# Gate logits from the raw rows with centred weights, gather norms on ScalarE, transposes inside products

## What is computed

```python
def moe(x):                                   # x: layer norm of the rows
    logits = x @ W_gate + b_gate              # 8 experts
    _, top_idx = top_k(logits, 2)
    y_all = relu(einsum('bsd,edh->bseh', x, W_e) + b_e)
    return take_along_axis(y_all, top_idx[..., None], axis=2).mean(axis=2)

x = x + 0.5 * moe(layernorm(x))
x = x + attention(layernorm(x))               # one head of width 128, softmax
x = x + 0.5 * moe(layernorm(x))
```

## Time and profile before

| what | value |
|---|---|
| runs, device time | median 271.39 us of 3 (270.65 to 272.92) |
| profiled execution, first to last instruction | 270.3 us; the median of the runs is 1.1 us above it |
| TensorE (PE) busy | 237.3 us, 88% |
| VectorE (DVE) busy | 168.9 us, 62% |
| GpSimd (POOL) busy | 118.9 us, 44% |
| ScalarE (ACT) busy | 103.1 us, 38% |
| chain that ended last | PE 59%, DVE 14%, DMA 10%, issue 6%, ACT 4% |
| mean granted TensorE clock | 0.985 of full |

### The profile page before, as it was taken

The page is one execution under the profiler, slowest core; times in us unless marked ns, Lnnn a source line. Parts: engine busy times, 40 slices in busy tenths (PEclk is TensorE's granted clock), DMA queues, the critical chain, the costliest instruction groups (busy, mean ns, idle before and its releaser), DMA issues.

```text
span 270.3 us, 4837 instructions
## 1 busy us (share of the span) xinstructions
PE 237.3 (88%) x1307; PEld 176.9 (65%) x1308; DVE 168.9 (62%) x413; ACT 103.1 (38%) x184; POOL 118.9 (44%) x137
## 2 busy tenths in 40 slices
PE   6687679998999999989999897789989999999940
PEld 2353258776888888658777575266766888888730
DVE  3659778976354444766788988837943454444691
ACT  1986825654333333313335325023432433333300
POOL 4300456755565652324232610332475666664240
PEclk9999999999999999999999999999999999999985
DMA  7999589743875456144402022162164445537995
GB/s 234 380 390 410 196 316 395 305 146 134 271 215 145 133 156 221 33 141 155 155 1 80 0 81 78 32 202 80 53 219 136 157 130 157 163 128 203 347 333 197
DMA packets 22789, 49.38 MB, mean 183 GB/s; under 512 B 4332, under 2 KB 4972, under 8 KB 22512
## 3 DMA queue, kind: packets, MB, share of 16 engines
q1 hardware_dynamic: 13712, 26.55, 27.8%
q0 software_dynamic: 7360, 20.46, 23.8%
q10 hardware_dynamic: 1696, 2.11, 2.3%
HBM read 34.42 MB, written 18.35 MB: 195 GB/s over the span
## 4 chain that ended last, share of the span: by engine, by line
PE 59%; DVE 14%; DMA 10%; issue 6%; ACT 4%; DVEq 1%; POOL 1%; another core or an unknown queue 1%; SPq 0%; POOLq 0%; ACTq 0%
PE qk_ps L883 17%; PE y_ps L883 15%; PE qk_ps L957 5%; PE tp_ps L857 5%; PE tp_ps L791 4%; DVE wlo L363 3%; PE v_ps L968 3%; DMA xg<-xn_dram,tok 3%; DMA whi<-z_dram 2%; DMA xg_late<-xn_dram,tok 2%; DMA z_dram<-xn,place 2%; DVE row_hot L1203 1%; PE g_ps L804 1%; PE sp_ps L979 1%; DVE ypre L1338 1%
## 5 line engine op out<-in xcount | busy, mean ns | idle before, releaser
L515 POOL DMA_INDIRECT xg<-xn_dram,tok x23 | 24.8, 1080 | 28.9 <-DVE tok L1252 17.7
L523 POOL DMA_INDIRECT z_dram<-yrow,place x23 | 25.8, 1123 | 24.2 <-ACT yrow L659 15.1
L515 POOL DMA_INDIRECT xg_late<-xn_dram,tok x23 | 22.6, 981 | 28.7 <-DVE tok L1252 13.2
L1330 DVE TENSOR_TENSOR xt_lo_late<-tp_ps,xt_hi_late 128x512 fp32r<-128x512 f32 x23 | 15.9, 692 | 26.2 <-ACT xt_hi_late L649 18.5
L659 ACT ACTIVATE yrow<-ypre 128x512 f32<-128x512 f32 x22 | 13.9, 633 | 43.6 <-DVE ypre L1338 35.6
L1330 DVE TENSOR_TENSOR xt_lo<-tp_ps,xt_hi 128x512 fp32r<-128x512 f32 x23 | 15.9, 691 | 20.4 <-ACT xt_hi L649 14.2
L523 POOL DMA_INDIRECT z_dram<-xn,place x16 | 17.1, 1071 | 20.2 <-ACT xn L659 15.0
L508 POOL TENSOR_TENSOR rstd<-var_eps,neg_half 128x2 f32<-128x2 f32 x12 | 8.8, 734 | 30.6 <-DVE var_eps L1111 30.5
L363 DVE TENSOR_TENSOR wlo<-raw,whi 128x1024 fp32r<-128x1024 f32 x16 | 19.0, 1217 | 1.5 <-POOL behind L543 0.9
L659 ACT ACTIVATE xn<-ypre_late 128x512 f32<-128x512 f32 x14 | 8.9, 633 | 25.6 <-DVE ypre_late L1338 24.0
L1104 DVE BATCH_NORM_STATS2 stats<-x 128x6 f32<-128x512 f32 x24 | 15.9, 686 | 3.9 <-DMA x<-in_L_attn_x_dram 3.7
(11 more groups left out here) (183 smaller groups left out, 532.1 us busy)
## 6 DMA issues: line engine op xcount, KB each, us to landing
raw<-in_L_ffn_W_e_dram SPq DMA_DIRECT2D x16, 512.0 KB, 9.4
z_rows<-z_dram SPq DMA_DIRECT2D x6, 512.0 KB, 4.5
x<-in_L_attn_x_dram SPq DMA_DIRECT2D x8, 256.0 KB, 4.3
be_bc<-in_L_ffn_b_e_dram SPq DMA_DIRECT2D x2, 1024.0 KB, 12.9
xn_dram<-xn ACTq DMA_DIRECT2D x8, 256.0 KB, 2.0
whi<-z_dram SPq DMA_DIRECT2D x4, 512.0 KB, 7.1
wlo<-z_dram SPq DMA_DIRECT2D x4, 512.0 KB, 8.3
out_dram<-x SPq DMA_DIRECT2D x8, 256.0 KB
```

The costliest lines, as they stand in the source:

```text
L515: pool.indirect_dma_start(out=xg_at(f, t % XG), out_offset=None, in_=xn_dram[f][0:T - S if f and t < NA else T, :], in_offset=bass.Indirec ...
L523: pool.indirect_dma_start(out=z_dram[f][:, :], out_offset=bass.IndirectOffsetOnAxis(ap=place[:, t:t + 1], axis=0), in_=yrow_at(f, t % YB), ...
L1330: dve.tensor_tensor(xt_lo_at(f, t % 2), tp_ps[(n0 + t) % 2][:], xt_hi_at(f, t % 2).bitcast(F32), ALU.subtract).then_inc(xt_made, 1)
```

## The change

1. **Gate from raw x.** The products of x with gate weights minus their column mean are the products of the centred rows; so TensorE transposes the rows of x themselves (`transpose_xn`), and rstd multiplies the logits in `choose`, where the bias is added too. The mean of the weights comes from four small products (`sum_gate_weights`), VectorE subtracts it once (`centre_gate_weights`). In `fold_logits` a product with a 0/1 matrix `fold` sums the four parts and transposes in one, so `choose` reads 8 columns a tile. The logits of the four batches of the first block stand in four PSUM banks.
2. **Norms.** All norms for the gathers are ScalarE's, behind the gate copies (`normalise_batch`), with their stores; eps and offset are GpSimd's. Norms for attention stay on VectorE.
3. **Order.** In the first block the counts stand behind all folds; there are fewer warm-ups between batches; SyncE loads six halves ahead of the stores; nine high and four low splits stand ahead of the experts, and one high split behind the first `xt_hi`. The transposes of tiles 1 to 3 of the first block stand inside the products before them. In the end of attention gate work is spread between quarters of `project_qk`.

The core of the diff:

```diff
-        HI_AHEAD = 10
-        LO_AHEAD = 5
-        LO_IN_TILE = [2, 2, 2, 2, 1, 2]
-
+        LATE_GATHERS = 3
+
+
+        HI_AHEAD = 9
+        LO_AHEAD = 4
+        LO_IN_TILE = [2, 2, 2, 2, 2, 2]
+
+        LOAD_FIRST = 6
...
                 s = n % MR
                 pool.wait_ge(var_made, n // TB + 1)
                 if n >= MR:
-                    pool.wait_ge(xn_made, n - MR + TB)
+                    done = gate_norms(n - MR + TB)
+                    pool.wait_ge(xg_made, done)
+                    if n - MR + TB > done:
+                        pool.wait_ge(xn_made, n - MR + TB - done)
+                if kind != "att":
+                    link(pool.tensor_scalar(var_eps[:, s:s + TB], mv[:, s:s + TB, 1], EPS, None, ALU.add))
                 pool.tensor_tensor(rstd[:, s:s + TB], var_eps[:, s:s + TB], neg_half[:], ALU.pow
                                    ).then_inc(rstd_made, 1)
+                if kind != "att":
+                    pool.wait_ge(rstd_made, n // TB + 1)
+                    link(pool.tensor_tensor(off[:, s:s + TB], mv[:, s:s + TB, 0], rstd[:, s:s + TB], ALU.mult))
+                    pool.tensor_scalar(off[:, s:s + TB], off[:, s:s + TB], -1.0, None, ALU.mult
+                                       ).then_inc(off_made, 1)
...
+            def normalise(f, i):
+
+                m = norm_no[(f"g{f}", i)]
+                s = m % MR
+                before_it = last_in_slot(m)
+                if before_it is not None:
+                    if norms[before_it][0] == "att":
+                        act.wait_ge(tp_full, use_no[norms[before_it]] + 1)
+                    if stores_from(xn_slot(m), m):
+                        act.wait_ge(xn_stored[xn_slot(m)], 16 * stores_from(xn_slot(m), m))
+                act.wait_ge(off_made, (f * NT + i) // TB + 1)
+                act.activation(xn_at(m), x[:, i, :], ACT.Identity, bias=off[:, s:s + 1],
+                               scale=rstd[:, s:s + 1]).then_inc(xg_made, 1)
...
+            def normalise_batch(f, b):
                 for i in range(TB * b, TB * (b + 1)):
+                    normalise(f, i)
+                if f:
+                    for i in range(TB * b, TB * (b + 1)):
+                        store_xn(i)
...
+                else:
+                    split_hi(hi_left.pop(0))
...
-            for i in range(TB):
-                normalise(i)
-            act.wait_ge(gate_in, 32)
             for b in range(B):
-                for i in range(TB * (b + 1), min(TB * (b + 2), NT)):
-                    normalise(i)
+                copy_gate(0, b)
                 if b:
                     copy_logits(0, b - 1)
-                copy_gate(0, b)
-                if b == B - 2:
-                    split_hi(his.pop(0))
+                if b < 2:
+                    normalise_batch(0, b)
             copy_logits(0, B - 1)
-            while len(his) > 5:
+            while len(his) > 6:
...
             copy_prob(b - 1)
+            copy_gate(1, b - 2, 0, 1)
             copy_ot(b - 1)
-            copy_gate(1, b - 2)
+            copy_gate(1, b - 2, 1, 2)
             copy_logits(1, b - 2)
-            copy_qk(b)
+            normalise_batch(1, b - 2)
             copy_gate(1, b - 1)
             copy_logits(1, b - 1)
+            normalise(1, TB * (b - 1))
+            copy_qk(b)
+            normalise(1, TB * (b - 1) + 1)
+            for i in range(TB * (b - 1), TB * b):
+                store_xn(i)
...
-                    pe.wait_ge(xn_made, m + 1)
+                    if kind == "att":
+                        pe.wait_ge(xn_made, i + 1)
+                        rows = xn_at(m)
+                    elif kind == "g0":
+                        pe.wait_ge(x_in_sem[i], 16)
+                        rows = x[:, i, :]
+                    else:
+                        pe.wait_ge(x_att, i + 1)
+                        rows = x[:, i, :]
...
+            def sum_gate_weights():
+
+                for c in range(NC):
+                    last = pe.matmul(wg_mean, mean_w[:], wg[:, c, 0:E], start=(c == 0), stop=(c == NC - 1))
+                last.then_inc(gate_summed, 1)
+
+            def fold_logits(f, b):
+
                 pe.wait_ge(gate_copied, f * B + b + 1)
                 for i in range(TB):
-                    last = pe.transpose(logit_ps[:, i, :, :].rearrange("p c q -> p (c q)"),
-                                        logit_t[:, i * P:(i + 1) * P], ident[:])
+                    last = pe.matmul(logits_at(f, b, i), logit_t[:, i * P:(i + 1) * P], fold[:],
+                                     start=True, stop=True)
...
-                    if f == 0 and t == 0:
-                        next_transposes(1)
+                    if f == 0 and t < LATE_GATHERS:
+                        next_transposes(t + 1)
+                    if f and t == NA - 1:
+                        next_transposes(t + 1)
+
+                def inside_high(t):
+
                     if f and t == 0:
                         transpose_xn("g1", B - 1)
-                    if f and t == NA - 1:
-                        next_transposes(t + 1)
-
-                def inside_high(t):
-
                     if f and t == 1:
-                        transpose_logits(1, B - 1)
+                        fold_logits(1, B - 1)
                     if f and t == 3:
                         token_list(2)
 
                 def tile(t):
-                    if t and t + 1 < NS and not (f and t in (1, NA - 1)):
+                    late = (0, 1, NA - 1) if f else range(LATE_GATHERS)
+                    if t + 1 < NS and t not in late:
...
-            warm_up(12)
+            warm_up(6)
             for b in range(B):
                 transpose_xn("g0", b)
-                if b > 1:
-                    count(0, b - 2)
                 if b:
-                    warm_up(2, sp_ps)
-                    transpose_logits(0, b - 1)
+                    pe.wait_ge(fold_made, 1)
+                    fold_logits(0, b - 1)
                 else:
-                    warm_up(3)
                     pe.wait_ge(gate_in, 32)
+                    sum_gate_weights()
+                    warm_up(2)
+                    pe.wait_ge(gate_centred, 1)
                 gate(0, b)
-            count(0, B - 2)
-            transpose_logits(0, B - 1)
-            warm_up(4, sp_ps)
-            count(0, B - 1)
-            warm_up(12, sp_ps)
+            fold_logits(0, B - 1)
+            warm_up(6, sp_ps)
+            for b in range(B):
+                count(0, b)
+            warm_up(14, sp_ps)
...
-            transpose_logits(1, b - 3)
+            fold_logits(1, b - 3)
             transpose_prob(b - 1)
+            transpose_xn("g1", b - 2)
             mix_v(b - 1)
+            count(1, b - 3)
             project_out(b - 1)
-            transpose_xn("g1", b - 2)
-            count(1, b - 3)
-            project_qk(b, 0, 1)
             gate(1, b - 2)
-            project_qk(b, 1, 2)
-            transpose_logits(1, b - 2)
+            project_qk(b, 0, 2)
             transpose_xn("g1", b - 1)
+            fold_logits(1, b - 2)
+            project_qk(b, 2, NC)
+            gate(1, b - 1)
+            project_qk(b, NC, NC + 2)
+            count(1, b - 2)
+            fold_logits(1, b - 1)
+            project_qk(b, NC + 2, 2 * NC)
             scores(b)
-            count(1, b - 2)
-            gate(1, b - 1)
-            transpose_logits(1, b - 1)
+            count(1, b - 1)
             transpose_prob(b)
-            warm_up(3, y0_ps)
-            count(1, b - 1)
...
+            def centre_gate_weights():
+
+                dve.wait_ge(gate_summed, 1)
+                dve.tensor_tensor(wg[:, :, 0:E], wg[:, :, 0:E], wg_mean.unsqueeze(1).broadcast_to([P, NC, E]),
+                                  ALU.subtract).then_inc(gate_centred, 1)
...
+                for i in range(TB):
+                    scaled = dve.scalar_tensor_tensor(out=logit[:, i, :], in0=logits_at(f, b, i),
+                                                      scalar=rstd[:, s + i:s + i + 1], in1=bg_bc[:],
+                                                      op0=ALU.mult, op1=ALU.add)
+                    if i < TB - 1:
+                        first = step(scaled)
+                    else:
+                        scaled.then_inc(logit_read, 1)
...
+                if b == 0:
+                    centre_gate_weights()
             dve.wait_ge(const_made, CONSTS)
+            dve.wait_ge(gate_in, 32)
             choose(0, 0)
             choose(0, 1)
-            split_lo(dve, 0, lo_made)
             choose(0, 2)
             split_rank(0, 0, 2)
+            choose(0, 3)
             row_hots(0, 0, 2)
-            choose(0, 3)
             places(0, B)
             tile_starts(0)
             slots(0)
             tokens(0)
             tile_experts(0)
-            split_lo(dve, 1, lo_made)
             dve.wait_ge(first_issued, 1)
-            for n in range(2, LO_AHEAD):
+            for n in range(LO_AHEAD):
...
```

(8 more changed lines are left out.)

131 lines of the change are left out of this document (71 added, 60 removed).

## The result

| | kernel before | changed kernel |
|---|---|---|
| median of 4 runs, us | 271.17 | 279.62 |
| lowest to highest, us | 270.65 to 272.92 | 278.46 to 281.37 |
| profiled execution: its time / its span, us | not on record / 270.3 | 278.46 / 276.6 |
| mean granted TensorE clock in it | 0.985 | 0.958 |

The ratio is 1.028, with a 95% interval of 1.023 to 1.034: the change makes the kernel 8 us slower. I had forecast 271.2 us, and nothing above 273.4 was in my range.

What follows compares the result with a forecast made beforehand. Bound: chain through head, first gather and experts, TensorE alone from product 7. -0.4 (head) -0.3 (first tiles) +0.5 (attention) = -0.2 on the 270.3 span: 270.1, plus 1.1 to the median: 271.2 us; range 270 to 272.5, wider 268.4 to 273.4.

Steps and rivals of the forecast that it cites:

- -0.4 at the first gather: Head: logits about 3 us earlier shrink to 0.4 us gained at the first gather, issued at 29.7 us.
- Bounds and views: Reading of the trace: whatever is gained or lost ahead of product 7 (62.43 us) counts fully at the end.
- The first gate, 7.75: Head: first gate product no longer waits for norms and starts at 7.75 us instead of 11.40.
- Gates 3.1 apart: Head: from the second gate on, a serial loop of gate, transposes, copy, logits and fold takes 3.1 us a batch.
- Last fold done at 18.6, pick at 20.25: Head: folds end at 18.6 us, then warm-ups and counts; VectorE's first rank pick at 20.25 instead of 20.66.
- Pick to gather: Head: the same pieces from first rank pick to gather in another order; choice 0.1 us longer, last-count wait 0.1 shorter.
- Stores and loads: Head: later norms end the loads near 31.5 us, crossing the first gather; up to 0.6 us, covered by slack.
- First tiles: First expert tiles: early transposes put bias 1 at 13.2 us behind the gather instead of 13.82; 0.3 us gained.
- Attention, +0.5: End of attention: scores 1.8 us later, projection 6.1 behind them, second part's gather 0.5 us later; bounds -0.3 to +1.3.
- Rival (c): Head: TensorE's clock falls to 1.2 GHz in gaps left by removed warm-ups; +4 us at the gather, 275 us; chance 0.07.
- Rival (a): Mainly the head gives more: prompt offsets, shorter loop, loads not crossing the gather, ranks deciding the list; 268.3 us; chance 0.22.
- Rival (b): First tiles hang on loads and splits that come no earlier, so head and tiles give 0; 271.9 us; chance 0.2.

Runs made afterwards that it cites:

- e2_tail: Changed kernel with warm-up products added in TensorE's gaps at the end of attention; ratio 1.017 to the kernel before.
- e8_bias_late: Changed kernel with the gate-bias broadcast issued later, behind ScalarE's first pair of gate copies, on its own semaphore; ratio 1.025 to the kernel before.
- b2_before_counts: Kernel before with only the counts of batches 0 to 2 moved behind the last logit transposes and six warm-ups; ratio 1.009.
- e5_counts: Changed kernel with the counts put back where the kernel before has them; ratio 1.024 to the kernel before.
- e9_norms_counts: Changed kernel with batch 2's norms and the counts both moved back into the head's loop; ratio 1.016 to the kernel before.
- e10_four: Changed kernel with batch 2's norms and counts back in the loop, late bias load, and warm-ups at the end of attention; ratio 1.022 to the kernel before.
- e1_head: Changed kernel with warm-up products added in the head's gaps, ahead of the folds; ratio 1.025 to the kernel before.
- e14_all_late_one: e13_all without the early transposes inside products 1 and 2; ratio 1.002 to the kernel before.
- e12_five: e5_counts with all ten weight halves ahead of the norm stores, late bias load, warm-ups in head and end of attention; ratio 1.016 to the kernel before.
- e13_all: Changed kernel, all norms and counts in loop, eight halves first, late bias load, warm-ups in head and attention's end, ScalarE's end reordered; ratio 1.004 to kernel before.

## Why the prediction was wrong

Two terms of the sum failed: -0.4 at the first gather, which measured +2.85, and +0.5 at the end of attention, which measured +3.43. The third, -0.3 for the first tiles, measured +0.64.

**Bounds and views.** That what is lost ahead of product 7 counts fully was right: the 2.85 us lost at the first gather were all there at the first projection of attention (3.49 late).

**The first gate, 7.75.** Measured 8.81. What the working left out was the load, which TensorE waited for (0.53 us), and that its start at half rate can last longer: the eight transposes took 1.92 us here and 1.29 in e2_tail, which had its gate at 7.62 with the load in place. That e8_bias_late came to 7.76 is in part luck. I listed what the change adds and did not price this 4 KB broadcast at all. Put into the kernel before it costs 2.25 us at the first gather by itself. The trough itself was open to no row of the trace before; that the change adds a DMA among the first loads was plain.

**Offset at 7.5, 0.25 an operation.** Right: GpSimd's add and two products took 0.19 to 0.25, the offset was ready at 7.25.

**Gates 3.1 apart.** Measured 3.34. The fold takes 0.58 us (0.61 for the last), not "at most the 0.38 of the logit transposes that it replaces": its two products show as four records, the two transposes as two.

**Last fold done at 18.6, pick at 20.25.** The fold was done at 20.6: 1.06 from the first gate, the rest from the longer steps. From there to the pick I had 1.65 us and it took 2.7: the six warm-ups stand in the chain with 2.0 at the falling clock instead of 1.4, and the counts behind them with 0.65 instead of 0.2. So the pick was 3.0 us late. This is the step that failed in the head: the counts were put behind all of this, and every term ahead of them (first gate, gate steps, warm-ups, the counts themselves) was too small or missing, so the 0.4 us that I let them gain became 2.6 lost. What their place alone is worth b2_before_counts shows: 2.5 us at the pick and 3.2 at the gather.

**Pick to gather.** 9.71 in place of 9.47 before: the list stood behind fourteen warm-ups at half rate, 0.5 us, less what VectorE's order gave.

**Stores and loads.** I wrote "up to 0.6", covered by slack. In the changed kernel nothing of it shows, but only because its gather came so late. With the gather in time (e5_counts) the first part takes 3.9 us more. The mechanism, a gather that crosses the loads, was named, but its size was missed: the norms end at 22.7, not 21.4, the DMA share is 0.58 in 20 to 22.5, the bias load's trough had made the loads late already, and TensorE's clock falls while it waits. e9_norms_counts and e10_four put 3.2 us on the bias load; what the late norms cost by themselves is not shown.

**First tiles.** Bias 0 at +9.56 (forecast +9.4), bias 1 at +13.15 (forecast 13.2 to 13.5): right. It was worth nothing in the changed kernel, as the step from bias 1 to bias 2 took 4.51 in place of 3.65; a part of that (0.95 us) stands in the trace as issue and not as a wait, and I leave its cause open.

**Attention, +0.5.** Measured +3.43. Counted from the first projection, the scores came 2.5 us later (I had 1.8); ScalarE's two store issues took 1.39 there and not 2 x 0.33. But the sentence "with less ahead of it 6.1" is what failed: the projection stood 7.52 us behind the scores (6.12 in e2_tail, where the clock is full), and the second gather stood 3.73 behind that (2.81 in e2_tail), another 0.9. With the warm-ups and gates gone from between scores and mixing, TensorE idled 1.85 us, its clock fell, and transposes, mixing and projection ran at 1.2 GHz. e2_tail puts 2.4 us of this profile's loss on that, 1.8 on the average of all profiles, and order takes the rest.

**The rivals.** Rival (c) is the one that happened, at a chance of 0.07. Its condition, "if the granted clock leaves 1.00 before the counts", came true: 0.54 at 21 to 22 us, counts from 22.4. Its price was not the one I gave: the gates kept their pace at full clock, and what suffered was the warm-ups behind them, 1.35 us by e1_head. So (c) explains only a part of the loss in the head; the same fall at the end of attention, which I had not looked for, cost more. My argument against it was one window of 1.10 busy of 2.50 that kept 1.00. A single window followed by busy ones said nothing of a row of four: 1.33, 1.33, 2.17 and 1.17 of 2.50 from 10 to 20 us were followed by the fall. The Trainium skill, "TensorE: Matmul & The Clock Gate", section "HAM oscillation — how this bites in real kernels", warns that a TensorE that keeps waiting is set back to half clock and begins its next burst cold. The traces of the changed kernel, of b2_before_counts and of e2_tail agree with it, and I had given it too little weight against one row. Rival (a) fell with the counts. Rival (b), first tiles that hang on the loads, could not show in the changed kernel, whose gather came too late; with the gather early (e5_counts) it was so, and with all repairs (1.002 and 1.004) head and tiles give nothing, as it had said: the first projection stands at 119.56 in e14_all_late_one and at 119.65 before.

## What to carry to other kernels

When a change takes work off a critical path, look for what then heads the queue behind it: here the counts, the norm stores, the weights and a small load were each within a few microseconds of being next, and every repair alone showed another. Warm-up products and small matmuls between waits are part of the schedule; if they are moved, say for every stretch what TensorE does between its waits, at the end of a phase too. And price each added DMA by where in the stream of loads it stands, not by its bytes.

## What the runs showed of the hardware

A broadcast of 32 bytes to each of 128 partitions, issued among the first loads, held the rest back: the DMA share fell to 0.46 in 3.75 to 6.25 us, 103 GB/s in place of 347, and a 256 KB tile of x came 2.26 us late. The share falls by more than half, so for the greater part the engines stood idle and weren't busy with small pieces. The Trainium skill, "DMA: Bandwidth & Descriptors", section "Specifications", says that transfers under 512 bytes don't reach line rate; that explains a slow transfer of its own, and no run here shows why the others stop. Issued at 6.6 to 6.9 us instead, it left a trough at 11 to 12 us in four of the five kernels that have it so (139 to 176 GB/s in e10_four, e12_five, e13_all and e14_all_late_one). It landed 6.1 to 6.8 us after its issue, and in all but e13_all VectorE's first choice waited 1.04 to 1.64 us for it.

TensorE starts at half rate, and how long differs from one execution to the next of the same kernel. In the profile of the changed kernel the first gate took 0.64 us, in the second profile of it 1.08, with the sums at 1.80 in place of 1.07; yet the granted clock reads 1.00 in both from 5 to 10 us. At this program's start the length of a known product tells the rate, not that column. The fourth gate stood at 18.84 in the one and 20.27 in the other.

The last scatter of the output took GpSimd 1.10 to 1.44 us in 8 of the 20 profiles of all kernels here, 2.60 in one, and 3.81 to 3.85 in eleven, two of them the kernel before with one edit:

```profile
266.05 3.81 POOL L550 DMA_INDIRECT z_dram<-xn,place  x1 [2.15 <-ACT xn L697]
```

This one is of e8_bias_late; the changed kernel has 1.40 for the same row. It stands in the chain and makes a part of the differences in the table's last column: the mean there is 99.3 us for the eleven profiles with the long scatter and 97.8 for the eight with the short one, but the eight alone lie between 96.51 and 100.00. No edit here decides it, its cause is open, and it is one reason why a single profile's end says little.
